# Attention of eight image groups run as one stream of 128 steps

## The chip, the core and the metric

The kernel runs on one core of one Trainium2 chip. The core has five engines that each work through a program of their own, in order: TensorE (PE in the rows, its weight loads PEld), VectorE (DVE), ScalarE (ACT), GpSimd (POOL) and SyncE (SP), which here only issues DMAs. They wait for each other by semaphores alone. TensorE writes to PSUM, eight banks of 128x512 fp32. The metric is the device time of one launch in microseconds (us), the median over runs.

## The reference

```python
proj = einsum('bnf,df->bnd', patchify(x, 16), W) + b          # 32 images, 36 patches of 768 pixels
h = concat([cls, proj], 1) + pos_enc                          # 37 tokens of 256
h = concat([h, txt], 1)                                       # 114 tokens per image
n = layernorm(h)
q, k, v = n @ Wq, n @ Wk, n @ Wv                              # 16 heads of 64
attn = softmax(causal(q k^T / 8)) ; out = attn v
h = h + (n + out @ Wo)
y = moe(layernorm(h))                                         # 8 experts, top 2, capacity 570, gelu MLP of 1024
return h + y
```

All is fp32. Products that need the full accuracy are made in three passes over high and low parts (`halves`: hi*hi, hi*lo, lo*hi); scores, transposes and attn*v are plain fp32.

## The kernel before

The 32 images are taken in 8 groups of 4 (456 tokens). After a prologue (weights split, group 0 embedded and normalised, its V, and its first Q and K) comes the attention phase, and then the eight experts one after the other, which the change does not touch.

**Inside a group.** 16 steps (`PAIRS`), each for two heads and two of the four images: TensorE makes four score matrices (`scores`), VectorE adds the mask and takes the row maximum (L983) and the bias (L987), ScalarE takes the exponential with its row sum (L706), VectorE inverts the sum (L991), GpSimd multiplies `pr` by it (L573), TensorE transposes the four (`transpose_probs`, `pT_bank`), ScalarE copies them to `pT` (L700), TensorE multiplies by V (`weigh_values`, `o_bank`), and ScalarE and VectorE store the high and low parts `oT_hi`, `oT_lo` (L696, L784). The transposes of a step are made two steps later and the products with V three steps later, so that a group has 16 + 3 rounds of the loop: in the first two no transposes, in the last three no scores.

**Other work, put between the steps of a group by fixed numbers.** In the first 13 rounds a chunk of the projections Q or K of this group for a later step (128x456, six matmuls, `project`); `E` (the embedded patches of the next group transposed), `Y` and `L` (the normalised output of the last group transposed, and the router's logits), `X` (tokens of the next group transposed) and V of the next group (8 blocks of six 512-wide matmuls, `project_v`). Behind the last round stand `embed` of the group after the next (32 matmuls into a score bank), `count_places`, the output projection `project_o` of the group (96 matmuls, 256 wide) and then Q0, K0 and Q1 of the next. All these small jobs go round three PSUM banks: `claim` waits until the job three places before was emptied by ScalarE or VectorE.

**The residual** `hx = hraw + xn` of a group is one buffer. GpSimd writes it in two halves (L583), the first only when the output projection of the last group has been taken.

**The pixels.** SyncE waits for both halves of `hx` (they free `hraw`), loads the text of the next group, then the pixels of the group after it (12 DMAs, L398), waits for them and shifts them in SBUF with two more (L406). ScalarE's `pack` (L645) waits for these and reorders the pixels for `embed`. In the kernel before it stands in step 10 of a group.

**Dispatch.** The router's result of a group is computed by VectorE in six parts (`route`), and GpSimd writes its rows to DRAM by 8 indirect DMAs (`dispatch`, L554), all of them between two groups.

Of the kernel before, what the change touches and what calls it, by code (L numbers as in the profile page):

```python
# [17 lines left out]
F32 = mybir.dt.float32  # L18
# [14 lines left out]
D = 256  # L33
# [37 lines left out]
def build(nc, x, txt, tokW, tok_b, cls_token, pos_enc, Wq, Wk, Wv, Wo,  # L71
          router_w, router_b, w1, b1, w2, b2, out, slots):
    ctx = ExitStack()
    with ctx:
# [41 lines left out]
        hx = place("hx", [T, GB, D])  # L116
# [13 lines left out]
        x2T = nc.alloc_sbuf_tensor_at("x2T", [128, KC, GT], F32, offset=x2T_at)  # L130
        rows = [place(f"rows{i}", [T, GB, ROW]) for i in range(2)]
# [66 lines left out]
        def psum(name):  # L198
# [17 lines left out]
        embedded, embT_done, packed = sem("embedded"), sem("embT_done"), sem("packed")  # L216
# [24 lines left out]
        START = ([("W", "d")] * 4 + [("E", "d")] * 2 + [("X", "ad")] * 2  # L241
                 + [("V", "a"), ("V", "d")] * GB + [("Q", "d"), ("K", "a"), ("Q", "d"), ("B", "d")])
# [9 lines left out]
        STATS2, MOMENTS2, NORM2 = {1: (0, 1), 2: (2, 3)}, 3, {5: (0, 1), 6: (2, 3)}  # L252
        STATS1, MOMENTS1, NORM1 = {7: (0, 1), 8: (2, 3)}, 8, {10: (0, 1), 11: (2, 3)}
        AT_RSTD1, AT_RSTD2 = 9, 4
        AT_PACK = 10

        ROUTE_AT = {AT_L + 3: 1, PAIRS: 2, PAIRS + 1: 3, PAIRS + 2: 4}

        LAST_QK = PAIRS - 3

        def next_qk(n):

            return "KQ"[n % 2], n // 2 + 1 + n % 2

        def body_jobs(first, last):
            jobs = []
            for n in range(PAIRS + 3):
                if n < LAST_QK:
                    jobs.append(next_qk(n) + (("a", "d")[n % 2],))
                if not last and n == AT_E:  # L270
                    jobs += [("E", 0, "d"), ("E", 1, "d")]
                if not first and n == AT_Y:
                    jobs += [("Y", 0, "a"), ("Y", 1, "d")]
                if not first and n == AT_L:
                    jobs.append(("L", 0, "d"))
                if not last and n == AT_X:
                    jobs += [("X", 0, "ad"), ("X", 1, "ad")]
                if not last:
                    jobs += [("V", 2 * b, "a") for b in V_FIRST.get(n, ())]
                    jobs += [("V", 2 * b + 1, "d") for b in V_SECOND.get(n, ())]  # L280
            if not first:
                jobs.append(("C", 0, "d"))
            jobs += [("O", 0, "d"), ("O", 1, "d")]
            if not last:
                jobs += [("Q", 0, "d"), ("K", 0, "a"), ("Q", 1, "d")]
            return jobs

        START_JOBS = []
        seen = {}
        for name, by in START:  # L290
            START_JOBS.append((name, seen.get(name, 0), by))
            seen[name] = seen.get(name, 0) + 1
        END_JOBS = [("Y", 0, "a"), ("Y", 1, "d"), ("L", 0, "d"), ("C", 0, "d")]
        FIRST, STEADY, LAST = body_jobs(True, False), body_jobs(False, False), body_jobs(False, True)
# [3 lines left out]

        ALL_JOBS = START_JOBS + FIRST + STEADY * (G - 2) + LAST + END_JOBS

        class Jobs:


            def __init__(self, where):
                self.seq = ALL_JOBS
                if where == "start":
                    self.at = 0
                elif where == "end":
                    self.at = len(ALL_JOBS) - len(END_JOBS)
                else:  # L310
                    self.at = len(START_JOBS) + (len(FIRST) + (where - 1) * len(STEADY) if where else 0)

            def index(self, name, k):
                for i in range(self.at, len(self.seq)):
                    if self.seq[i][:2] == (name, k):
                        return i
                raise KeyError((name, k))

            def bank(self, name, k):
                return bank[self.index(name, k) % len(bank)]  # L320

            def total(self, i, engine=None):
                return count(self.seq[:i + 1], engine)

            def last_before(self, name, k):

                return max(i for i in range(self.at) if self.seq[i][:2] == (name, k))

            def filled(self, name, k):
                return self.total(self.index(name, k))  # L330

            def emptied(self, i):

                sems = {"a": act_drained, "d": dve_drained}
                return [(sems[e], self.total(i, e)) for e in self.seq[i][2]]

            def drained(self, name, k):
                return self.emptied(self.index(name, k))

            def bank_free(self, name, k):  # L340

                i = self.index(name, k) - len(bank)
                return self.emptied(i) if i >= 0 else []


# [25 lines left out]
        def pair(g, n):  # L371
            return g * PAIRS + n
# [18 lines left out]
        def _(sp):  # L391
# [48 lines left out]
            def body(g, first=False, last=False):  # L440
                jobs = Jobs(g)
                if not last:
                    sp.wait_ge(hx_done, 2 * g + 2)
                    load_text(g + 1)
                if g < G - 2:
                    sp.wait_ge(packed, g + 2)
                    load_pixels(g + 2)
                if first:
                    clear_slots()
                if not first:  # L450
                    wait_all(sp, jobs.emptied(jobs.last_before("O", 1)))
                    set_out(g - 1)

            body(0, first=True)
            for g in range(1, G - 2):
                body(g)
            body(G - 2)
            body(G - 1, last=True)
            jobs = Jobs(G - 1)
            wait_all(sp, jobs.drained("O", 1))  # L460
# [15 lines left out]
            jobs = Jobs("end")  # L476
            wait_all(sp, [(filled, jobs.filled("L", 0))])
# [19 lines left out]
        def _(pool):  # L497
# [68 lines left out]
            def body(g, first=False, last=False):  # L566
                for n in range(PAIRS + 1):
                    if n >= 1:

                        m = n - 1  # L570
                        after((recip_done, pair(g, n)))
                        for i in range(4):
                            p = pool.tensor_scalar(pr[:, m % 4, i, :], pr[:, m % 4, i, :], rc[:, m % 4, i:i + 1], 1.0, ALU.mult, ALU.mult)  # L573
                        p.then_inc(normed, 1)
                    if n in (0, 1):

                        if first and n == 0:
                            after((xn_done, GB))
                        elif n == 0:
                            jobs = Jobs(g)  # L580
                            after((xn_done, GB * (g + 1)), *jobs.emptied(jobs.last_before("O", 1)))
                        b = slice(2 * n, 2 * n + 2)
                        pool.tensor_tensor(hx[:, b, :], hraw[:, b, :], xn[:, b, :], ALU.add).then_inc(hx_done, 1)  # L583
                    if n == AT_RSTD2 and not first:
                        rstd(g - 1, vareps2, rstd2_done, ve2, rstd2)
                    if n == AT_RSTD1 and not last:
                        rstd(g + 1, vareps1, rstd1_done, ve1, rstd1)
                if not first:
                    for i in range(TOPK * GB):
                        dispatch(g - 1, i)  # L590

            body(0, first=True)
            for g in range(1, G - 1):
                body(g)
            body(G - 1, last=True)
# [18 lines left out]
        def _(act):  # L614
# [7 lines left out]
            def drain(jobs, name, k, dst, src, **kw):  # L622
                act.wait_ge(filled, jobs.filled(name, k))
                act.activation(dst, src, ACT.Copy, **kw).then_inc(act_drained, 1)  # L624

            def drain_x(jobs, k):
                drain(jobs, "X", k, xT_hi[:, k, :], jobs.bank("X", k)[:, 0:GT])

            def drain_k(jobs, c):
                drain(jobs, "K", c, kT[:, c % 2, :], jobs.bank("K", c)[:, 0:GT])  # L630

            def drain_v(jobs, b):
                drain(jobs, "V", 2 * b, vv[:, b, 0:512], jobs.bank("V", 2 * b)[0:T, :])

            def drain_y(jobs):
                drain(jobs, "Y", 0, x2T[:, 0, :], jobs.bank("Y", 0)[:, 0:GT])
# [20 lines left out]
            for k in range(KC):  # L657
                drain_x(jobs, k)
# [746 lines left out]
```

## Time and profile before

| | us |
|---|---|
| median of 3 runs | 954.19 (951.41 to 954.93) |
| the profiled execution | 953.52 |
| its span | 951.6 |
| first scores of group 0 | 51.82 |
| first scores of groups 1 and 2 | 133.48 and 214.02 |
| first scores of group 7 | 612.25 |
| output projection of group 7 starts | 665.84 |
| TensorE busy | 869.6 (91% of the span) |
| VectorE, ScalarE, GpSimd busy | 556.2, 516.0, 370.5 |

Times in the rows are us from the start of the span. A row of the timeline is a run of equal instructions: its start, how long it lasted, engine, line, operation, tiles and count, and in brackets how long the engine stood idle before it and which instruction ended that. Matmuls overlap: the next one starts before the last has ended, so that the step from start to start is what one costs. The PEclk column is the TensorE clock that was granted, 1.00 for 2.4 GHz and 0.50 for 1.2 GHz.

### The profile page before, as it was taken

The page shows a single profiled execution, that of the slowest core. Times are in us where ns is not written, and L with a number is a line of the kernel's source. Part 1 is how long each engine was busy: PE and PEld are TensorE (multiplying, and loading weights), DVE is VectorE, ACT ScalarE, POOL GpSimd, SP SyncE. Part 2 cuts the span into 40 slices and gives each one's busy share as a digit, 9 for nine tenths or more (in the row PEclk, how much of TensorE's full clock was granted, in tenths as well). Part 3 has the DMA queues.
Part 4 walks back from the last instruction along what each step waited for, and adds up shares of the span by engine and source line. Part 5 has one row for each costly group of instructions (what it writes and reads, how often), then busy time and mean ns, then how long its engine had stood idle before and what let it go on. Part 6 is the DMA issues. An engine that isn't in the chain of part 4 may idle for free.

```text
span 951.6 us, 19817 instructions
## 1 busy us (share of the span) xinstructions
PE 869.6 (91%) x6897; PEld 754.2 (79%) x6897; DVE 556.2 (58%) x2433; ACT 516.0 (54%) x1686; POOL 370.5 (39%) x677
## 2 busy tenths in 40 slices
PE   4898999999999999999999999997708999999996
PEld 4676787797788778779777877875708999999996
DVE  3566347528645753863775485476236767777761
ACT  3368438807824961880684386186016555565551
POOL 2134225345425424543542653554430333322333
PEclk8799899999999999999999999998758999999999
DMA  8224302012002101200200200100135655444322
GB/s 252 50 58 132 98 13 60 2 41 74 1 8 65 43 1 42 71 2 22 68 16 1 59 9 2 38 2 1 24 100 179 158 117 134 102 121 121 83 26 25
DMA packets 61908, 57.64 MB, mean 61 GB/s; under 512 B 26784, under 2 KB 56652, under 8 KB 61697
## 3 DMA queue, kind: packets, MB, share of 16 engines
q1 hardware_dynamic: 41170, 45.15, 15.5%
q0 software_dynamic: 18944, 9.76, 6.5%
q10 hardware_dynamic: 1696, 1.49, 0.6%
q8 instruction: 55, 0.90, 0.4%
q14 instruction: 43, 0.34, 0.1%
HBM read 34.25 MB, written 21.89 MB: 59 GB/s over the span
## 4 chain that ended last, share of the span: by engine, by line
PE 82%; DVE 4%; POOL 4%; issue 4%; ACT 3%; DMA 1%; SPq 1%; POOLq 0%; DVEq 0%; ACTq 0%
PE bank L380 14%; PE bank L382 13%; PE bank L381 13%; PE pT_bank L1241 6%; PE score_bank L1232 6%; PE o_bank L1252 6%; PE score_bank L1130 4%; POOL pr L573 2%; PE o_bank L381 2%; PE o_bank L382 2%; PE o_bank L380 2%; PE score_bank L380 2%; PE score_bank L381 2%; PE score_bank L382 2%; ACT pr L706 2%
## 5 line engine op out<-in xcount | busy, mean ns | idle before, releaser
L573 POOL TENSOR_SCALAR pr<-pr,rc 114x114 f32<-114x114 f32 x512 | 179.7, 371 | 233.7 <-DVE rc L991 233.7
L706 ACT ACTIVATE pr<-sm,nb 114x114 f32<-114x114 f32 x512 | 192.1, 379 | 22.6 <-DVE nb L987 21.2
L983 DVE CUSTOM_DVE_ANT_0 sm<-score_bank,mask 114x114 f32<-114x114 f32 x512 | 110.5, 272 | 55.2 <-PE score_bank L1232 55.2
L604 POOL DMA_INDIRECT out_dram<-yout,dest x40 | 74.0, 1849 | 163.0 <-ACT yout L758 161.5
L554 POOL DMA_INDIRECT slots_dram<-rows,slot x64 | 72.8, 1137 | 128.2 <-DVE slot L950 93.3
L624 ACT ACTIVATE kT<-bank 128x456 f32<-128x456 f32 x64 | 34.1, 532 | 146.8 <-PE bank L382 146.8
L380 PE MATMUL bank<-xT_hi,wqkv_hi 128*128 128x456 f32 x256 | 103.5, 404 | 0.0
L1232 PEld LDWEIGHTS score_bank<-kT,qT 64*114 64x114 f32 x1024 | 62.1, 177 | 45.5 <-issue 35.3
L706 ACT ACTIVATION_READ_ACCUMULATOR pr<-sm,nb 114x1 f32 x512 | 97.0, 189 | 0.0
L381 PE MATMUL bank<-xT_lo,wqkv_hi 128*128 128x456 f32 x256 | 94.3, 368 | 0.0
L382 PE MATMUL bank<-xT_hi,wqkv_lo 128*128 128x456 f32 x256 | 94.3, 368 | 0.0
L1232 PE MATMUL score_bank<-kT,qT 64*114 64x114 f32 x1024 | 84.8, 284 | 9.1 <-DVE mx L983 6.0
L1241 PE MATMUL pT_bank<-ident,pr 114*114 114x114 f32 x512 | 78.1, 276 | 10.2 <-POOL pr L573 10.2
L700 ACT ACTIVATE pT<-pT_bank 114x456 f32<-114x456 f32 x128 | 70.5, 551 | 23.4 <-PE pT_bank L1241 23.2
L1252 PE MATMUL o_bank<-pT,vv 114*64 114x114 f32 x1024 | 79.2, 276 | 2.3 <-ACT pT L700 2.1
L1241 PEld LDWEIGHTS pT_bank<-ident,pr 114*114 114x114 f32 x512 | 49.6, 136 | 30.4 <-POOL pr L573 14.0
L380 PE MATMUL bank<-wo_hi,oT_hi 128*114 128x256 f32 x256 | 73.4, 287 | 0.0
L382 PE MATMUL bank<-wo_hi,oT_lo 128*114 128x256 f32 x256 | 72.8, 284 | 0.0
L381 PE MATMUL bank<-wo_lo,oT_hi 128*114 128x256 f32 x256 | 72.7, 284 | 0.0
L696 ACT ACTIVATE oT_hi<-o_bank 128x228 fp32r<-128x228 f32 x128 | 45.7, 357 | 47.3 <-PE o_bank L1252 47.3
L1252 PEld LDWEIGHTS o_bank<-pT,vv 114*64 114x64 f32 x1024 | 50.9, 137 | 22.9 <-issue 8.1
L784 DVE TENSOR_TENSOR oT_lo<-o_bank,oT_hi 128x228 fp32r<-128x228 f32 x128 | 47.9, 374 | 34.0 <-ACT oT_hi L696 33.5
(198 smaller groups left out, 2228.1 us busy)
## 6 DMA issues: line engine op xcount, KB each, us to landing
stage_a<-in_L_ffn_w_dram SPq DMA_DIRECT2D x8, 1024.0 KB, 5.0
stage_b<-in_L_ffn_w_dram SPq DMA_DIRECT2D x8, 1024.0 KB, 7.1
slots_dram<-fill SPq DMA_DIRECT2D x8, 605.6 KB
xs<-slots_dram SPq DMA_DIRECT2D x8, 605.6 KB
pix<-in_x_dram SPq DMA_DIRECT2D x96, 36.0 KB, 2.3
hraw<-in_txt_dram SPq DMA_DIRECT2D x8, 308.0 KB
out_dram<-h SPq DMA_DIRECT2D x8, 308.0 KB
pix<-pix SPq DMA_DIRECT2D x7, 216.0 KB, 2.6
```

What stands on the lines that cost most here:

```text
L380: pe.matmul(out_ap, a[0], b[0], start=start, stop=False)
L381: pe.matmul(out_ap, a[0], b[1], start=False, stop=False)
L382: return pe.matmul(out_ap, a[1], b[0], start=False, stop=stop)
L554: pool.indirect_dma_start(slots, bass.IndirectOffsetOnAxis(ap=slot[:, j, b:b + 1], axis=0), rows[k % 2][:, b, :], None, bounds_check=E * C ...
L573: p = pool.tensor_scalar(pr[:, m % 4, i, :], pr[:, m % 4, i, :], rc[:, m % 4, i:i + 1], 1.0, ALU.mult, ALU.mult)
L604: pool.indirect_dma_start(out, bass.IndirectOffsetOnAxis(ap=dest[e % 2][:, t:t + 1], axis=0), yout[:, t, :], None, compute_op=ALU.add).the ...
L700: act.activation(pT[:, m % 2, :, :], pT_bank[0:T, 0:4 * T].rearrange("p (i q) -> p i q", i=4), ACT.Copy).then_inc(pT_copied, 1)
L706: a = act.activation(pr[:, n % 4, i, :], sm[:, n % 2, i, :], ACT.Exp, bias=nb[:, n % 2, i:i + 1], scale=SCALE, accum_out=rs[:, n % 4, i:i ...
L983: m = dve.tensor_tensor_reduce(sm[:, n % 2, i, :], score_bank[i % 2][0:T, i // 2 * T:(i // 2 + 1) * T], mask[:, :], 1.0, NEG, ALU.add, ALU ...
L1232: m = pe.matmul(score_bank[h][0:T, b * T:(b + 1) * T], qT[head, c % 2, tokens], kT[head, c % 2, tokens], start=True, stop=True)
L1241: m = pe.transpose(pT_bank[0:T, i * T:(i + 1) * T], pr[:, n % 4, i, :], ident[0:T, 0:T])
L1252: m = pe.matmul(o_bank[n % 2][h * DK:(h + 1) * DK, b * T:(b + 1) * T], vv[:, b0 + b, v0:v0 + DK], pT[:, n % 2, 2 * b + h, :], start=True, ...
```

## The change

The loops over groups and over the steps in one are replaced by one loop over 128 steps N (group g, step n), plus four rounds to drain it. There are no rounds without scores between two groups, and the transposes of a step are now made three steps later (`LAG_T`), the products with V four (`LAG_O`).

- A chunk of Q or K stands in every one of the 16 steps; those of steps 13, 14 and 15 are of the next group.
- The second halves of V (`V2` below, 4 blocks) of a group are made in its own steps 5 to 8; of the first halves three stand in steps 14 and 15 of the group before and one in step 0. In the prologue only the first halves of group 0 are left.
- The output projection of the last group stands in steps 4 and 5, half each. Its input `oT` is still one buffer, so that in these two steps ScalarE's and VectorE's high and low parts (`late`) wait for it and stand at the end of the step.
- `embed` is in step 9, in one of the three banks. `E` is in step 6, `Y` in 10, `L` in 11, `X` in 13.
- `pack` is moved from step 10 to step 4, behind the late part. Both halves of `hx` are now written in steps 1 and 2, into two buffers in turn.
- The dispatches of a group stand in steps 4 to 11 of the group after the next, one in each.

TensorE makes the same matmuls as before, and no engine has other instructions than before.

```diff
-        AT_E, AT_Y, AT_L, AT_X = 3, 8, 12, 13
-        V_FIRST = {AT_X + 1: (0,), AT_X + 2: (1, 2), AT_X + 3: (3,)}
-        V_SECOND = {PAIRS + 1: (0, 1), PAIRS + 2: (2, 3)}
-        AT_PACK = 10
+        LAG_T, LAG_O = 3, 4
+        AT_O, AT_V2, AT_E, AT_M, AT_Y, AT_L, AT_X = 4, 5, 6, 9, 10, 11, 13
+        AT_PACK, AT_RSTD1, AT_RSTD2 = 4, 10, 8
+        NORM1 = {11: (0, 1), 12: (2, 3)}
...
-                    if n in (0, 1):
-                        if first and n == 0:
-                            after((xn_done, GB))
-                        elif n == 0:
-                            after((xn_done, GB * (g + 1)), *jobs.emptied(jobs.last_before("O", 1)))
+                if g < G and n in (1, 2):
+                    if n == 1:
+                        pool.wait_ge(xn_done, GB * (g + 1))
+                        if g > 1:
+                            wait_all(pool, drained("O", 2 * g - 3))
...
+                late = n in (LAG_O, LAG_O + 1)
+                if N >= LAG_O and not late:
+                    take_outputs(N - LAG_O)
+                if LAG_T <= N < STEPS + LAG_T:
+                    m = N - LAG_T
+                    act.wait_ge(pT_done, m + 1)
+                    act.activation(pT[:, m % 2, :, :], ...).then_inc(pT_copied, 1)
...
+                if N >= LAG_O and late:
+                    take_outputs(N - LAG_O)
+                if g + 2 < G and n == AT_PACK:
+                    pack(g + 2)
...
+            for N, g, n in steps():
+                if n == AT_X and g + 1 < G:
+                    transpose_tokens("X", g + 1, xn, xn_done)
+                if N < STEPS:
+                    scores(N)
+                if N >= LAG_O:
+                    weigh_values(N - LAG_O)
+                if LAG_T <= N < STEPS + LAG_T:
+                    transpose_probs(N - LAG_T)
+                if g < G:
+                    if chunk_at(g, n):
+                        project(*chunk_at(g, n))
+                    for f, b in value_jobs(g, n):
+                        project_v(f, b, 0)
+                    if n - AT_V2 in range(GB):
+                        project_v(g, n - AT_V2, 1)
+                    if n == AT_E and g + 1 < G:
+                        transpose_patches(g + 1)
+                    if n == AT_M and g + 2 < G:
+                        embed(g + 2)
+                    if g > 0:
...
+                        if n - AT_O in range(2):
+                            project_o(g - 1, n - AT_O)
```

TensorE at the start of a group, before: the last matmul of the output projection of group 0, then the last matmul of Q0, K0, Q1, and the first three steps of group 1 (L1232 scores, L1241 transposes, the rest a chunk of Q or K).

```order
L382 MATMUL bank<-wo_hi,oT_lo 114x256
...
L382 MATMUL bank<-xT_hi,wqkv_lo 128x456
L1232 MATMUL score_bank<-kT,qT 114x114 x4
L380 MATMUL bank<-xT_hi,wqkv_hi 128x456
...
L1232 MATMUL score_bank<-kT,qT 114x114 x4
L380 MATMUL bank<-xT_hi,wqkv_hi 128x456
...
L1232 MATMUL score_bank<-kT,qT 114x114 x4
L1241 MATMUL pT_bank<-ident,pr 114x114 x4
```

After: TensorE in step 5 of group 1, with the end of the output projection's first half before it, a chunk of K, one V2 block and the second half, and then the start of step 6.

```order
L361 MATMUL bank<-wo_hi,oT_lo 114x256
L1166 MATMUL score_bank<-kT,qT 114x114 x4
L1187 MATMUL o_bank<-pT,vv 64x114 x4
L1175 MATMUL pT_bank<-ident,pr 114x114 x4
L359 MATMUL bank<-xT_hi,wqkv_hi 128x456
...
L359 MATMUL bank<-wqkv_hi,xT_hi 114x512
...
L359 MATMUL bank<-wo_hi,oT_hi 114x256
...
L1166 MATMUL score_bank<-kT,qT 114x114 x4
```

The output projection has gone from between two groups, where nothing of attention stood beside it, into two steps with scores, products and transposes.

ScalarE in group 0, before: from the exponentials of step 9 past `pack` of group 2 (L645) into step 11.

```order
L700 ACTIVATE pT<-pT_bank 114x456
L706 ACTIVATE pr,rs<-sm,nb 114x114 x4
L696 ACTIVATE oT_hi<-o_bank 128x228
L700 ACTIVATE pT<-pT_bank 114x456
L706 ACTIVATE pr,rs<-sm,nb 114x114 x4
L645 ACTIVATE tok<-pix 96x1152
L624 ACTIVATE kT<-bank 128x456
```

After: from the exponentials of step 3 past the same `pack` (now L610) into step 5.

```order
L673 ACTIVATE pr,rs<-sm,nb 114x114 x4
L588 ACTIVATE kT<-bank 128x456
L667 ACTIVATE pT<-pT_bank 114x456
L673 ACTIVATE pr,rs<-sm,nb 114x114 x4
L648 ACTIVATE oT_hi<-o_bank 128x228
L610 ACTIVATE tok<-pix 96x1152
L667 ACTIVATE pT<-pT_bank 114x456
L673 ACTIVATE pr,rs<-sm,nb 114x114 x4
```

`pack` is six steps earlier in the group, and the copy of the transposed probabilities of step 2 now stands right behind it.

## Rows read from the trace of the kernel before

**Rows 1.** Busy time by engine over the stream of group 0 and of group 1
```profile
core 0: us, PE busy (x) PEld busy (x) DVE busy (x) ACT busy (x) POOL busy (x), PEclk, DMA share, GB/s
51.82:133.48 81.66, 78.27 (x610) 63.69 (x610) 39.01 (x209) 46.55 (x175) 25.91 (x67) 0.96 0.28 84
133.48:214.02 80.54, 78.14 (x635) 64.26 (x635) 47.33 (x252) 47.35 (x177) 36.22 (x76) 1.00 0.13 34
```

**Rows 2.** Timeline of TensorE in group 1: two of its idle times
```profile
169.14 0.66 PE L1232 MATMUL score_bank<-kT,qT 64*114 64x114 f32 x8 [0.51 <-ACT kT L624]
...
176.97 0.66 PE L1232 MATMUL score_bank<-kT,qT 64*114 64x114 f32 x8 [0.64 <-DVE mx L983]
```

**Rows 3.** Timeline of TensorE in group 1: one plain step, to the next scores
```profile
153.23 0.66 PE L1232 MATMUL score_bank<-kT,qT 64*114 64x114 f32 x8
153.81 0.61 PE L1252 MATMUL o_bank<-pT,vv 114*64 114x114 f32 x8
154.36 0.60 PE L1241 MATMUL pT_bank<-ident,pr 114*114 114x114 f32 x4
154.73 0.45 PE L380 MATMUL bank<-xT_hi,wqkv_hi 128*128 128x456 f32 x1
...
156.13 0.56 PE L1232 MATMUL score_bank<-kT,qT 64*114 64x114 f32 x6
```

**Rows 4.** Timeline of TensorE: starts of V blocks, L, X, embed and the output projection
```profile
41.96 0.39 PE L380 MATMUL bank<-wqkv_hi,xT_hi 128*114 128x512 f32 x1
...
43.35 0.40 PE L380 MATMUL bank<-wqkv_hi,xT_hi 128*114 128x512 f32 x1
...
172.06 1.67 PE L1265 MATMUL bank<-router_sb,x2T 128*114 128x8 f32 x16
173.59 1.08 PE L1150 MATMUL bank<-ident,xn 114*128 114x114 f32 x8
174.60 0.66 PE L1232 MATMUL score_bank<-kT,qT 64*114 64x114 f32 x8
...
194.76 4.08 PE L1130 MATMUL score_bank<-tok,embW 96*128 96x144 f32 x32
...
198.76 0.35 PE L380 MATMUL bank<-wo_hi,oT_hi 128*114 128x256 f32 x1
...
210.19 0.38 PE L380 MATMUL bank<-xT_hi,wqkv_hi 128*128 128x456 f32 x1
```

**Rows 5.** Timeline of all engines in group 0: residual, pixel DMAs and pack
```profile
55.90 1.40 POOL L573 TENSOR_SCALAR pr<-pr,rc 114x114 f32<-114x114 f32 x4 [20.59 <-DVE rc L991]
...
57.27 1.27 POOL L583 TENSOR_TENSOR hx<-hraw,xn 114x512 f32<-114x512 f32 x1
...
57.58 0.99 DVE L987 TENSOR_SCALAR nb<-mx 114x4 f32<-114x4 f32 x1
...
66.67 2.09 SPq L406 DMA_DIRECT2D pix<-pix  x2
...
84.07 2.19 ACT L645 ACTIVATE tok<-pix 96x1152 f32<-96x1152 f32 x1
```

**Rows 6.** DMA issues of the page: KB each, median us to landing
```profile
pix<-pix SPq DMA_DIRECT2D x7, 216.0 KB, 2.6
```

**Rows 7.** Timeline of TensorE in group 0: its longest idle time
```profile
94.38 1.12 PE L1232 MATMUL score_bank<-kT,qT 64*114 64x114 f32 x8 [2.11 <-DVE mx L983]
```

**Rows 8.** Busy time by engine in the stretches behind that idle time
```profile
94.30:98.00 3.70, 3.62 (x22) 2.99 (x23) 2.01 (x14) 2.53 (x11) 2.61 (x8) 0.50 0.42 130
98.00:102.00 4.00, 4.00 (x27) 2.75 (x25) 1.03 (x10) 2.46 (x11) 0.18 (x1) 0.68 0.42 131
```

**Rows 9.** Timeline of TensorE: scores of step 13 of group 7, last product, output projection
```profile
650.90 0.66 PE L1232 MATMUL score_bank<-kT,qT 64*114 64x114 f32 x8
...
662.76 1.03 PE L1252 MATMUL o_bank<-pT,vv 114*64 114x114 f32 x8 [0.64 <-ACT pT L700]
...
665.84 0.54 PE L380 MATMUL bank<-wo_hi,oT_hi 128*114 128x256 f32 x1
```

More of the change, by code:

```diff
@@ L296, in count @@
+        JOB_AT = {job[:2]: i for i, job in enumerate(JOBS)}
         def count(jobs, engine=None):
             return sum(1 for j in jobs if engine is None or engine in j[2])
[L299 to L343, printed above, removed]
@@ L369, in ebank_free, with steps @@
             return [{"H": (gelu_done, NF * f + n + 1), "S": (xs_done, NX * f + n + 1), "Y": (y_done, CT * f + n + 1)}[was]]
-        def pair(g, n):
-            return g * PAIRS + n
+        STEPS = PAIRS * G
+        def steps():
+            for N in range(STEPS + LAG_O):
+                yield (N,) + divmod(N, PAIRS)
         def wait_all(eng, waits):
@@ L596, in _ @@
+            for i in range(TOPK * GB):
+                dispatch(G - 2, i)
             rstd(G - 1, vareps2, rstd2_done, ve2, rstd2)
@@ L722, in _ @@
+            drain_y(G - 1)
             router_exp(G - 1)
@@ L1045, in _ @@
+                if N >= LAG_O and late:
+                    give_low_outputs(N - LAG_O)
+            for i in range(2):
+                drain_o(G - 1, i)
+                dve.wait_ge(dve_drained, drained_by("O", 2 * (G - 1) + i, "d"))
+                for b in (2 * i, 2 * i + 1):
+                    statistics(b, h2, st2, stats2)
             moments(G - 1, st2, mv2, stats2, moments2)
@@ new lines, in count_places, with scores @@
+            def count_places(k):
+                pe.wait_ge(routed, ROUTE_STEPS * k + sum(ROUTE_PARTS[:5]))
+                dst = claim("C", k)[0:T, 0:GB * E]
+                pe.matmul(dst, upto[:, :], chosen[:, :, :], start=True, stop=False)
+                pe.matmul(dst, ones[:, :], before[:, 0:GB, :], start=False, stop=True).then_inc(filled, 1)
+            def scores(N):
+                n = N % PAIRS
+                c, b0 = N // 2, 2 * (n % 2)
+                if b0 == 0:
+                    wait_all(pe, drained("K", c))
+                    wait_all(pe, drained("Q", c))
+                if N > 0:
+                    pe.wait_ge(max_done, N)
@@ new lines, in _ @@
+            wait_all(pe, drained("W", 3))
+            embed(0)
+            transpose_patches(0)
+            transpose_tokens("X", 0, xn, xn_done)
+            tokens_split(0)
+            pe.wait_ge(wv_lo, 1)
+            for b in range(GB):
+                project_v(0, b, 0)
+            pe.wait_ge(wk_lo, 1)
+            project("K", 0)
+            pe.wait_ge(wq_lo, 1)
+            project("Q", 0)
+            project("K", 1)
+            embed(1)
+            pe.wait_ge(b1_in, 16)
+            dst = claim("B", 0)
@@ L1297, in body @@
                         if n == AT_Y:
[L1298 to L1300 removed]
+                            transpose_tokens("Y", g - 1, rows[(g - 1) % 2], xn2_done)
                         if n == AT_L:
[L1302 to L1307 removed]
@@ L1308, in body @@
-                if not last and not (isinstance(g, int) and g == G - 2):
-                    embed(g + 2)
-                if not first:
-                    count_places(jobs, g - 1)
-                if first:
-                    pe.wait_ge(wo_lo_done, 1)
-                pe.wait_ge(o_lo, pair(g, PAIRS))
-                for k in range(2):
-                    project_o(jobs, k)
-                if not last:
-                    project(jobs, "Q", 0)
-                    project(jobs, "K", 0)
-                    project(jobs, "Q", 1)
@@ L1335, in e_claim @@
+                if n == AT_C and g > 1:
+                    count_places(g - 2)
+            for i in range(2):
+                project_o(G - 1, i)
+            transpose_tokens("Y", G - 1, rows[(G - 1) % 2], xn2_done)
+            logits(G - 1)
+            count_places(G - 1)
             def e_claim(name, e, k):
```

697 lines of the change are left out of this document (301 added, 396 removed).

## The prediction

> **What bounds the kernel now.** I read the page first: TensorE is busy for 91% of the span and no other engine for more than 58%. Then the windows by stage. From the first scores of group 1 to those of group 2 TensorE is busy for 78.14 us of 80.54 at the full clock, beside 47.3 us of VectorE and of ScalarE and 36.2 us of GpSimd [rows 1]. So in the attention phase only TensorE counts. An idle 2.4 us is the first thing that a better order can give back in a group. The timeline shows what ends it: in two of its four pieces, 0.51 us until ScalarE has stored K and 0.64 us until VectorE has taken the row maxima [rows 2]. The other two wait for GpSimd's `pr`. Group 0 is worse: 3.4 us idle and a mean clock of 0.96 [rows 1].
>
> **What a group costs when nothing waits.** Start to start, a plain step is 156.13 - 153.23 = 2.90 us: scores 0.58, products with V 0.55, transposes 0.37, a chunk 1.40 [rows 3]. A V block is 43.35 - 41.96 = 1.39, `embed` and the two small matmuls behind it 198.76 - 194.76 = 4.00, the output projection 210.19 - 198.76 = 11.43, L 1.53, X 1.01 [rows 4]. Y and E have X's shape or nearly, and I take 0.85 for each; behind a chunk L, X, E or Y saves a change back of some 0.08. The new group holds 16 plain steps 46.4, 8 V blocks 11.1, `embed` and C 4.0, output projection 11.4, and L, X, Y, E 4.1 together: 77.0 us. That is 3.5 below 80.54: 2.4 is the idle time, 1.1 the changes of operand and of tile in the three rounds without scores and in the first two steps, which are gone.
>
> **What the new order puts in its place.** I followed each queue through the steps with the durations above.
> - Step 6: the second E job needs the bank that Q of the same step filled, and VectorE stores that only in step 7. It begins step 6 late, since the low part of step 5's output waits for the second half of the output projection; then come a V2 block, an output half, the maxima, a low part and two statistics, together about 5.1 us behind the start of step 6, where TensorE asks at 4.6: 0.5 us.
> - Steps 12 to 14: VectorE normalises the last two images in step 12 behind the router's first part, about 0.5 us too late for X in step 13, and K of step 13 waits some 0.3 us for the low part of X. The maxima of step 13 are late as well, but a chunk now stands ahead of the next scores, so the 0.64 us [rows 2] are covered.
> - Steps 4 and 5: `oT` is single, so its writers wait for TensorE. Nothing on TensorE needs them before step 6, and each half projection is 5.7 us long.
>
> That makes 1.3 us a group. It is bounded by 0 (all covered) and by 3.5 (each of these queues is late by about as much as in the old order, and the gain is eaten). I take 1.3, since each part comes from a row-by-row count and VectorE has 30 us to spare in a group.
>
> The dispatches now run beside VectorE. While GpSimd added `hx` from 57.27 to 58.54, VectorE's `nb`, 4 elements wide, took 0.99 us and ended with it [rows 5]: the two block one another. At most that adds 1 us to a step's VectorE work in 8 steps of 16; in steps 4 to 11 TensorE mostly needs 3.6 us or more, and the transposes have a whole step more of slack, so I put it at 0 with the bound above. By the Trainium skill ("SBUF — State Buffer", section Who interferes with whom) the shared port pair is an exclusive lock, and a DMA from GpSimd's queue can wait for VectorE to get its descriptors written; by that rule the dispatch could be late as well as `nb`, each time by one VectorE instruction. The sum by the row has `nb` alone late; by the rule the dispatches are too, and both leave it at 940.8, since GpSimd has 40 us spare in a group and nobody in the phase waits for a dispatch; only the bound of 3.5 us a group would be reached more easily.
>
> **The early pack in group 0.** This is the large term against the change. The pixels for group 2 are asked for when both halves of `hx` are written. Before, the second half ended at 57.27 + 1.27 = 58.54, 6.7 us after the first scores at 51.82. Now it stands behind `pr` of step 1 as well as the first half: 1.40 + 1.27 more, and ends 9.4 to 9.5 us after them. From there the load and the shift were issued by 66.67 + 2.09 = 68.76 [rows 5]; landing takes 2.6 from an issue [rows 6], the last of which began at about 68.2, so the pixels are there 12.2 us after the residual: 21.7 us after the first scores. `pack` then takes 2.19 [rows 5], and the copy of step 2's transposes behind it 0.55: 24.4 us. TensorE wants that copy in step 6. It gets there after three steps of 2.04 (scores and a chunk, with the changes between them), one of 2.36 with transposes, one of 2.90, one of 4.29 with V2, and the scores of step 6: 16.3 us. It stands for 8.1 us. `pack` was in step 10 before, at 84.07, 13 us after its pixels were in.
>
> After 2.11 us of idle time [rows 7] the granted clock was 0.50 for 3.7 us and 0.68 for the next 4.0 [rows 8], which is 3.7 x 0.50 + 4.0 x 0.32 = 3.1 us of work; part of the slow stretch is also ScalarE catching up, so I take 2.5. Together 10.6 us, bounds 0 (the pixels come sooner) and 14.
>
> In groups 1 to 5 the same chain ends about 24 us after the first scores, but there `pack` stands beside the output projection: step 6 starts 31.7 us after them (4.3 + 3 x 2.9 + 8.6 + 10.0). After 2.7 us for `pack` and copy some 5 us are left. I cost it at nothing; if that cover goes, the price is what comes above 5 us, per group.
>
> **The sum.** The prologue has four V blocks less: 4 x 1.39 = 5.6, first scores at 51.82 - 5.56 = 46.3. VectorE's weight splits still lie beside the rest. Group 0: 46.4, less 3 x 0.37 and 4 x 0.55 for the empty pipeline, plus 7 V blocks 9.7, E 0.9, `embed` 3.9, X 0.8: 58.5. Then groups 1 to 5 at 77.0, group 6 without `embed` 73.1, and group 7 to its step 13: 13 x 2.9 + 5 x 1.39 + 11.4 + Y, L, C 2.3 = 58.4. So these scores start at 46.3 + 58.5 + 385.0 + 73.1 + 58.4 = 621.3, plus 10.6 for the early pack, plus 6 x 1.3 + 0.5 for the waits: 640.2, against 650.90 [rows 9]: 10.7 earlier.
>
> The tail: the last three steps are bound by the chain through ScalarE and GpSimd as before. The output projection started at 665.84, 3.1 us behind the last products at 662.76 [rows 9], since it waited for the router's count and for the last low part. Now the count is a step earlier and the first half asks only for the last step but one: it starts when the products are done, about 2 us sooner. All behind it follows. The dispatches of group 6 still stand ahead there, but start sooner as well.
>
> In all 10.7 + 2.0 = 12.7 us less. The profiled execution took 953.52 (span 951.6 and 1.9 around it), 0.7 below the median 954.19. So its like would take 940.8, the median 941.5, and I say 941.5.
>
> **Rivals.**
> - *No stall in group 0.* The pixels come before TensorE needs the copy, or something I don't see hides it. For it: the DMA engines are lightly loaded. Against: it is SyncE's issue of 14 DMAs that takes the 10 us, not the bytes. 941.5 - 10.6 = 931. Chance 0.12.
> - *The waits move instead of going.* VectorE and ScalarE, in order, pass the late parts on, and dispatches block VectorE, so that a group loses the whole 3.5 us: 6 x 2.2 = 13 us back. 954.5, no change. For it: the three banks are tight in steps 5 to 7 and VectorE's queue there is full. Against: 30 us of slack a group. Chance 0.10; half of it on the way there (about 948) 0.08.
> - *Slower: the pack isn't covered in groups 1 to 5 either.* Place: step 6 of each, TensorE waiting for the copy behind `pack`. It decides once the pixels land over 5 us later than I reckon; each further us costs 5, and any gap of 2 us or more brings the clock's 3 us with it. At 8 us late: 5 x (3 + 2.5) = 28, 969. For it: group 0 does just this. Against: the load of each group is the same 14 DMAs, and the cover is made of the two halves of the output projection, whose length a row gives [rows 4]. Chance 0.06.
> - My forecast, 937 to 946 by itself: 0.64.
>
> The range that leaves out 2 in 10: 931 to 949. A measurement of this kernel tells 0.5%, 4.8 us, from no change. Faster than 949.4: 0.64 + 0.12 + 0.06 of the halfway case = 0.82; same (to 959) 0.12; slower 0.06.
>
> **What would show it.** First scores of group 0 at 46.3. An idle time of TensorE of 8 us ahead of the products of step 6 in group 0, released by ScalarE's copy with `pack` ahead of it, and the clock at 0.50 behind it. First scores of group to group 78.3 us apart, idle some 1.3, ended by VectorE in steps 6 and 13. In groups 1 to 5 `pack` ends before step 6. Output projection of group 7 right behind the last products. I am wrong if the groups are 80 us apart, if the large idle time returns in every group, or if group 0 has none.

## The result, and the profile after

| | before | after |
|---|---|---|
| median, runs on one chip | 954.02 (951.38 to 954.93), 7 runs | 947.86 (945.23 to 948.27), 7 runs |
| ratio | | 0.9939 [0.9923, 0.9955] |
| the profiled execution, its span | 953.52, 951.6 | 947.86, 945.7 |
| first scores of groups 0, 1, 2 | 51.82, 133.48, 214.02 | 46.76, 117.73, 195.83 |
| periods of groups 2 to 5, group 6 | 80.57, 75.96 | 78.92 to 78.99, 75.02 |
| scores of step 13 of group 7 | 650.90 | 645.93 |
| last product, output projection | 662.76, 665.84 | 660.16, 661.11 |

The change makes the kernel 6.2 us faster. The forecast of 941.5 is 12.5 below the same median, so the time lies inside the range but the gain is a little less than half of what was said.

The page of the kernel after; TensorE is busy for nearly as long as before (866.3 us against 869.6), in a span 5.9 us shorter:

```profile
span 945.7 us, 19862 instructions
...
PE 866.3 (92%) x6897; PEld 759.8 (80%) x6897; DVE 562.7 (60%) x2433; ACT 519.1 (55%) x1686; POOL 373.2 (39%) x677
```

The windows of groups 0, 1 and 2, from first scores to first scores, the view of [rows 1]:

```profile
46.76:117.73 70.97, 61.76 (x464) 48.94 (x463) 36.03 (x203) 42.54 (x166) 24.38 (x63) 0.93 0.32 97
117.73:195.83 78.10, 77.26 (x634) 64.64 (x633) 43.39 (x235) 47.80 (x177) 26.90 (x68) 1.00 0.09 23
195.83:274.75 78.92, 77.38 (x635) 64.91 (x634) 48.76 (x252) 47.84 (x177) 36.84 (x76) 1.00 0.13 35
```

TensorE's idle time fell from 2.4 us in a group of 80.5 to 0.8 in group 1 and 1.5 in group 2. Group 0 is 71 us long, but 9.2 of them are idle and its mean clock is 0.93. The waits view says what all of it was. These are all waits of TensorE from 46 to 646 us (engine, tile and line, who released it, us in total, times, longest):

```profile
PE o_bank L1187 <- ACT pT L667: 8.5, 1, 8.5
PE bank L359 <- issue: 5.8, 7, 0.8
PE score_bank L1166 <- DVE mx L951: 4.2, 6, 0.7
```

Three waits, 18.5 us, each always in the same place. The document goes through them one after the other.

**The single wait of 8.5 us** is in group 0, step 6. TensorE's timeline, then ScalarE's, then the windows behind the wait:

```profile
62.48 0.66 PE L1166 MATMUL score_bank<-kT,qT 64*114 64x114 f32 x8
71.61 1.03 PE L1187 MATMUL o_bank<-pT,vv 114*64 114x114 f32 x8 [8.48 <-ACT pT L667]
```

```profile
68.98 2.14 ACT L610 ACTIVATE tok<-pix 96x1152 f32<-96x1152 f32 x1 [9.32 <-DMA pix<-pix]
71.03 0.53 ACT L667 ACTIVATE pT<-pT_bank 114x456 f32<-114x456 f32 x1
```

```profile
71.61:74.50 2.89, 2.89 (x15) 2.50 (x16) 1.18 (x5) 2.79 (x12) 0.00 (x0) 0.50 0.41 133
74.50:78.00 3.50, 3.50 (x11) 2.60 (x10) 1.76 (x12) 1.60 (x8) 1.39 (x4) 0.58 0.42 132
78.00:82.00 4.00, 4.00 (x37) 3.29 (x35) 3.19 (x14) 1.73 (x7) 0.87 (x3) 1.00 0.42 131
```

The releaser named is the copy, but read one row up: what it copies was there before 62.48, and it stood behind `pack`, which waited 9.32 us for the pixels. The copy started 24.3 us behind the first scores and ended 24.8 us behind them. Afterwards TensorE ran at 1.2 GHz (0.50) and was back at 2.4 by 78.0: 2.9 x 0.50 + 3.5 x 0.42 = 2.9 us of work.

**The six waits of 0.70 us**, one in each of groups 2 to 7: TensorE, VectorE and GpSimd at the end of step 3 of group 2.

```profile
209.69 0.66 PE L1166 MATMUL score_bank<-kT,qT 64*114 64x114 f32 x8 [0.70 <-DVE mx L951]
```

```profile
207.19 0.17 DVE L904 SCALAR_TENSOR_TENSOR sl<-pick,ps__114 114x8 f32<-114x8 f32 x1
207.28 1.29 DVE L906 TENSOR_SCALAR over<-ps__114 114x8 f32<-114x8 f32 x1
208.60 0.17 DVE L908 SCALAR_TENSOR_TENSOR slot<-sl,over 114x8 int32<-114x8 f32 x1
208.68 0.27 DVE L951 CUSTOM_DVE_ANT_0 sm<-score_bank,mask 114x114 f32<-114x114 f32 x1
```

```profile
207.25 1.28 POOL L551 TENSOR_TENSOR hx<-hraw,xn 114x512 f32<-114x512 f32 x1
```

The router's fifth part stands ahead of the maxima in VectorE's step 3. Its `over`, 8 elements wide like its neighbours of 0.17, lasts 1.29 and ends when GpSimd's second half of `hx` does (208.57 and 208.53).

**The seven waits of 0.84 us** (0.73 in group 0) stand ahead of K of step 13 in groups 0 to 6. TensorE and VectorE in group 1:

```profile
184.45 0.45 PE L359 MATMUL bank<-xT_hi,wqkv_hi 128*128 128x456 f32 x1 [0.84 <-issue]
```

```profile
182.64 1.17 DVE L745 TENSOR_TENSOR xT_lo<-bank,xT_hi 128x456 fp32r<-128x456 f32 x2 [1.59 <-ACT xT_hi L588]
183.73 0.62 DVE L749 COPY qT<-bank 128x456 f32<-128x456 f32 x1
```

"Issue" says only that the profile names no releaser; the queues show it. K of step 13 takes the bank that Q of step 12 filled; VectorE was idle for 1.59 us, nearly all of it with that Q ready, since the low parts of X, which wait for ScalarE, stand ahead of it. K starts 0.10 us after the store of Q ends (183.73 + 0.62 = 184.35).

**The end of the stream.** TensorE from the scores of step 13 of group 7 on:

```profile
645.93 0.66 PE L1166 MATMUL score_bank<-kT,qT 64*114 64x114 f32 x8
...
649.38 0.66 PE L1166 MATMUL score_bank<-kT,qT 64*114 64x114 f32 x8
650.47 0.61 PE L1187 MATMUL o_bank<-pT,vv 114*64 114x114 f32 x8 [0.43 <-ACT pT L667]
...
652.64 0.61 PE L1187 MATMUL o_bank<-pT,vv 114*64 114x114 f32 x8 [1.03 <-ACT pT L667]
...
654.94 1.03 PE L1187 MATMUL o_bank<-pT,vv 114*64 114x114 f32 x8 [1.16 <-ACT pT L667]
...
657.55 1.03 PE L1187 MATMUL o_bank<-pT,vv 114*64 114x114 f32 x8 [0.64 <-ACT pT L667]
...
660.16 1.03 PE L1187 MATMUL o_bank<-pT,vv 114*64 114x114 f32 x8 [0.52 <-ACT pT L667]
...
661.11 0.56 PE L359 MATMUL bank<-wo_hi,oT_hi 128*114 128x256 f32 x1
```

From the start of the last scores to that of the last products it is 10.78 us, where the kernel before took 662.76 - 654.86 = 7.90: the stream now has four rounds to drain, not three, and in each the products wait for ScalarE's copy. The output projection then starts 0.95 us after the last products start, not 3.1 [rows 9].

### The profile page after: what moved, and what is told of

Same layout as the page of the kernel before. It is cut to its first block, busy times and chain, and to the rows that moved or that the text cites. A ratio compares the mean times of both kernels' runs of the same rounds, so it can differ in the third digit from the quotient of the medians.

```text
span 945.7 us, 19862 instructions
## 1 busy us (share of the span) xinstructions
PE 866.3 (92%) x6897; PEld 759.8 (80%) x6897; DVE 562.7 (60%) x2433; ACT 519.1 (55%) x1686; POOL 373.2 (39%) x677
## 3 DMA queue, kind: packets, MB, share of 16 engines
q1 hardware_dynamic: 41170, 45.15, 15.7%
## 4 chain that ended last, share of the span: by engine, by line
PE 83%; DVE 7%; issue 4%; DMA 2%; POOL 2%; ACT 1%; SPq 1%; POOLq 0%; DVEq 0%
PE bank L359 14%; PE bank L360 13%; PE bank L361 13%; PE score_bank L1166 7%; PE o_bank L1187 6%; PE pT_bank L1175 6%; PE bank L1081 4%; PE o_bank L360 2%; PE o_bank L361 2%; PE o_bank L359 2%; PE score_bank L359 2%; PE score_bank L360 2%; PE score_bank L361 2%; PE bank L1101 2%; DVE sm L951 2%
## 5 line engine op out<-in xcount | busy, mean ns | idle before, releaser
L359 PE MATMUL bank<-xT_hi,wqkv_hi 128*128 128x456 f32 x256 | 105.2, 411 | 5.8 <-issue 5.8
L524 POOL DMA_INDIRECT slots_dram<-rows,slot x64 | 75.6, 1181 | 36.1 <-DVE slot L908 19.8
L1175 PE MATMUL pT_bank<-ident,pr 114*114 114x114 f32 x512 | 78.5, 277 | 0.0
L1187 PEld LDWEIGHTS o_bank<-pT,vv 114*64 114x64 f32 x1024 | 51.4, 138 | 26.8 <-ACT pT L667 13.5
L359 PE MATMUL bank<-wo_hi,oT_hi 128*114 128x256 f32 x256 | 72.6, 284 | 0.0
L745 DVE TENSOR_TENSOR hid_lo<-gl,hid_hi 128x282 fp32r<-128x282 f32 (+1 forms) x128 | 58.4, 456 | 4.4
```

Source lines behind the costliest of these rows:

```text
L359: pe.matmul(out_ap, a[0], b[0], start=start, stop=False)
L524: pool.indirect_dma_start(slots, bass.IndirectOffsetOnAxis(ap=slot[:, j, b:b + 1], axis=0), rows[k % 2][:, b, :], None, bounds_check=E * C ...
L745: dve.tensor_tensor(lo, whole, hi.bitcast(F32), ALU.subtract).then_inc(done, 1)
L1175: p = pe.transpose(pT_bank[0:T, i * T:(i + 1) * T], pr[:, m % 4, i, :], ident[0:T, 0:T])
L1187: p = pe.matmul(o_bank[m % 2][h * DK:(h + 1) * DK, b * T:(b + 1) * T], vv[:, b0 + b, v0:v0 + DK], pT[:, m % 2, 2 * b + h, :], start=True, ...
```

## The experiments

All edit the kernel after. They ran on two chips, on which the kernel before took 954.02 us (experiments 1 to 4) and 952.34 us (5 to 8), so each is given by its ratio to the kernel before on the same chip; 0.0010 is 0.95 us, and the kernel after stands at 0.9939. Beside it stands what the trace of one execution gives from the first scores of group 0 to the end of the span, which leaves the prologue out: its length ran from 45.15 to 47.36 us over the nine traces of this order, with the same instructions in it but for experiment 5. The kernel after has 945.7 - 46.76 = 898.9 there.

**1. Pack of group 2 later, in group 0 alone.**

```diff
-                if g + 2 < G and n == AT_PACK:
+                if g + 2 < G and n == (8 if g == 0 else AT_PACK):
                     pack(g + 2)
```

> The changed kernel with one pack moved: that of group 2, which stands in group 0, from step 4 to step 8; the others stay in step 4. Theory (the copy behind the early pack holds TensorE, and the clock falls with it): the idle time of 8.5 us in step 6 of group 0 and the slow matmuls behind it go, 11 us in all, so 936.9 against 947.9; first scores of groups 0 and 1 about 60 us apart instead of 71. Rival (TensorE would have stood there anyway, for the load of the pixels or for ScalarE's backlog): the idle time only moves to step 9 or 10 and the time changes by less than 3 us.

Measured: 935.98 (935.39 to 937.38), ratio 0.9815 [0.98, 0.9831]: 11.9 us faster than the kernel after; by the trace 888.2, 10.7 less. The window of group 0, then TensorE's waits from 45 to 640 us:

```profile
47.17:106.86 59.69, 58.96 (x465) 46.89 (x464) 36.07 (x203) 42.62 (x166) 24.47 (x63) 1.00 0.35 105
```

```profile
PE bank L359 <- issue: 5.8, 7, 0.8
PE score_bank L1166 <- DVE mx L951: 4.3, 6, 0.7
PE o_bank L1187 <- ACT pT L667: 0.4, 1, 0.4
```

The large wait and the slow clock are gone, group 0 is 70.97 - 59.69 = 11.3 us shorter, and the two small waits are untouched (the last row is the first wait of the drain). So the wait did not move to a later step. Of the 11.3 the trace as a whole keeps 10.7: groups 1 to 6 together are 0.2 longer and the stretch behind the scores of step 13 of group 7 is 0.4 longer, which is no more than two executions may differ by.

**2. The store of Q ahead of the low parts of X on VectorE.**

```diff
-                    if n == AT_X and g + 1 < G:
-                        drain_x(g + 1)
                     if n % 2 == 1 and chunk_at(g, n - 1):
                         drain_q(chunk_at(g, n - 1)[1])
+                    if n == AT_X and g + 1 < G:
+                        drain_x(g + 1)
```

> The changed kernel with VectorE's queue of step 13 in another order: the chunk of Q made in step 12 is stored before the low parts of X and not behind them. Theory (TensorE's wait of 0.84 us ahead of K of step 13 is for this store): the wait falls to about 0.3 us in each of 7 groups, 3.8 us less, 944.1. Rival (it waits for the low part of X alone, which ScalarE's exponentials make late): 947.9, nothing changes.

Measured: 943.66 (941.92 to 945.35), ratio 0.9894 [0.9877, 0.991], 4.2 us faster than the kernel after; by the trace 895.2, 3.7 less. The waits are now `PE bank L359 <- issue: 2.0, 7, 0.3`, and the periods of groups 2 to 5 78.4 to 78.5. So it was the store of Q; the 0.3 left is K waiting for the low parts of X themselves (in group 2 they end at 262.21 and K starts at 262.31), the amount that the prediction had named.

**3. The router's fifth part behind the maxima.**

```diff
-                if n == AT_C + 1 and g > 1:
-                    route(g - 2, 5)
...
-                if g > 1 and n in ROUTE_NEXT and n != AT_C + 1:
+                if g > 1 and n in ROUTE_NEXT:
                     route(g - 2, ROUTE_NEXT[n])
```

> The changed kernel with the router's last part moved on VectorE from ahead of the maxima of step 3 to the end of step 3. Theory (this part, 1.0 us by itself and 2.1 with GpSimd's block, is what makes the scores of step 4 wait 0.70 us): the wait goes in groups 2 to 7, 6 x 0.7 = 4.2 us less, 943.7. Rival (VectorE's queue is late as a whole there, and the wait turns up in the next step or at the bank of the output projection): less than 1 us.

Measured: 942.99 (941.91 to 943.43), ratio 0.989 [0.9872, 0.9908], 4.9 us faster than the kernel after; by the trace 894.7, 4.3 less. The six waits are gone, the periods 78.2. In this kernel `over` has a mean of 0.16 us, and in its place `nb` of step 3 lasts 0.94 at 205.72, beside the same half of `hx`: the stretched instruction stays, on another victim that TensorE does not wait for.

**4. The drain with transposes ahead of products.** ScalarE's copy stands ahead of its high part there in the same way.

```diff
-                if N >= LAG_O:
+                if LAG_O <= N < STEPS:
                     weigh_values(N - LAG_O)
                 if LAG_T <= N < STEPS + LAG_T:
                     transpose_probs(N - LAG_T)
+                if N >= STEPS:
+                    weigh_values(N - LAG_O)
```

> The changed kernel with the four rounds behind the last scores in another order: transposes before products on TensorE, and the copy of the transposes before the output's high part on ScalarE. Theory (the one step more of lag made the drain a chain of four times product, transpose, copy, 2.2 to 2.6 us each, 10.8 us from the last scores to the last product against 7.9 before): the last product comes 7.9 to 8.5 us after the last scores, 2.5 us less, 945.4. Rival (the chain through exponentials and GpSimd sets the end of the drain): nothing changes, 947.9.

Measured: 946.05 (944.9 to 947.36), ratio 0.9921 [0.9906, 0.9937], 1.8 us faster than the kernel after, within the uncertainty of the two; by the trace 897.9, 1.1 less. From the last scores to the last product it takes 656.74 - 647.23 = 9.51 us, 1.27 less. The drain is still 1.6 longer than before, and 7.9 to 8.5 was expected: the transposes now wait for ScalarE's copy in their turn (1.11 and 0.95 us), and from 652.65 on a set of them takes 0.98 instead of 0.60, so the slow clock is still there.

**5. The halves of the residual a step earlier.** Experiment 3 doesn't tell the length of part five from GpSimd's hold on VectorE. This one leaves VectorE's order alone.

```diff
-                if g < G and n in (1, 2):
+                if g < G and n in (0, 1):
...
-                    b = slice(2 * n - 2, 2 * n)
+                    b = slice(2 * n, 2 * n + 2)
                     pool.tensor_tensor(hx[g % 2][:, b, :], hraw[:, b, :], xn[:, b, :], ALU.add).then_inc(hx_done, 1)
```

> The two halves of the residual hx are added by GpSimd in steps 0 and 1 of a group instead of 1 and 2; nothing else moves. It tests two things. First, group 0: the pixels for group 2 are asked for when the second half is written, so that the idle time of TensorE ahead of the products of step 6 should shrink from 8.48 us by what the residual comes earlier, one step of about 2.8 us, to about 5.7; the slow clock behind it stays. If the stall were set by the length of the transfer or by pack itself, it would stay at 8.5. Second, groups 2 to 7: the wait of 0.70 us of the scores of step 4 for the row maxima. My theory is that the last GpSimd half (207.25, 1.28 us) stretches VectorE's 8-wide over from 0.17 to 1.29 us; then over takes about 0.17 again, and the wait is gone (6 x 0.7 = 4.2 us). The rival is that the router's fifth part, standing ahead of the maxima, is late by its own length: then the wait stays at 0.7. Theory: 947.9 - 2.8 - 4.2 = 941. Rival: 945. If neither moves: 948.

Measured: 940.1 (939.29 to 941.65) against 952.34, ratio 0.9871 [0.9853, 0.9889], 6.5 us faster than the kernel after; by the trace 891.5, 7.5 less. TensorE's waits from 45 to 640 us, and `over` of group 2:

```profile
PE o_bank L1187 <- ACT pT L667: 6.2, 1, 6.2
PE bank L359 <- issue: 5.8, 7, 0.8
```

```profile
203.44 0.17 DVE L906 TENSOR_SCALAR over<-ps__114 114x8 f32<-114x8 f32 x1
```

Both parts of the theory hold. Part five still stands ahead of the maxima, and the 0.70 us are gone with GpSimd's addition. The addition now meets another instruction of VectorE, which TensorE doesn't wait for:

```profile
195.46 1.28 POOL L551 TENSOR_TENSOR hx<-hraw,xn 114x512 f32<-114x512 f32 x1
195.48 1.31 DVE L885 TENSOR_TENSOR oh<-io,pick 114x32 f32<-114x32 f32 x1
```

And the stall of group 0 shrank by 2.3 us (5.7 was expected, 6.19 measured) as the residual came earlier: its second half ends 52.67 - 45.95 = 6.7 us behind the first scores instead of 56.29 - 46.76 = 9.5. So the stall is dated by the residual, not by the length of the transfer alone. The 2.8 did not come back whole, since SyncE's twelve loads of pixels took 8.52 us instead of 8.04.

**6. The four edits of 1 to 4 together.**

> Four edits together: pack of group 2 in step 8 of group 0, VectorE's store of Q ahead of the low parts of X in step 13, the router's fifth part at the end of VectorE's step 3, and the drain with transposes ahead of products. Alone they gave 11.9, 4.2, 4.9 and 1.8 us against the kernel after the change (947.86). If they act in different places and nothing else comes to bind, they add: 947.9 - 22.8 = 925.1, ratio to the kernel before 0.970. The rival is that they share part of their gain (a wait that one removes was given back at the next by the other): then 929 to 932. Periods of the groups from 2 on about 77.7 us.

Measured: 927.85 (927.32 to 929.21) against 952.34, ratio 0.9741 [0.9726, 0.9756]. That is 18.9 us below the kernel after, and 2.6% faster than before. By the medians (0.9741 x 954.02 = 929.3) that is the rival's figure, 3.9 short of the 22.8. The trace says otherwise: 925.3 - 45.57 = 879.7, 19.2 less, where the four alone gave 10.7 + 3.7 + 4.3 + 1.1 = 19.8. By the traces they add within 0.6 us, and the sum of four differences of medians was too large. The periods of groups 2 to 5 are 77.6 to 77.7, as expected. The window of group 2:

```profile
182.41:260.11 77.70, 77.40 (x635) 64.89 (x635) 48.72 (x252) 48.04 (x177) 36.94 (x76) 1.00 0.13 36
```

An idle 0.30 us is left in a group, the K of step 13.

**7. All dispatches of a group in step 5.**

```diff
-                if 1 < g < G and n - AT_DISPATCH in range(TOPK * GB):
-                    dispatch(g - 2, n - AT_DISPATCH)
+                if 1 < g < G and n == AT_DISPATCH + 1:
+                    for i in range(TOPK * GB):
+                        dispatch(g - 2, i)
```

> The eight indirect DMAs of a group's dispatch all stand in step 5 on GpSimd instead of one in each of steps 4 to 11. Each occupies GpSimd for 1.2 to 1.4 us in the trace of the kernel after the change. The prediction put the dispatches at no cost. If that is right, this kernel takes the same time, 947.9, within 1.5 us: the burst of about 10 us lies beside the two halves of the output projection, and the pr of step 4 comes some 3 us late where the transposes are three steps away. The rival is that each dispatch beside the steps holds VectorE up for about a microsecond and so delays maxima in steps 6 to 11 of five or six groups: then taking seven of the eight away from these steps gives back 3 to 10 us (938 to 945).

Measured: 946.79 (946.02 to 948.69) against 952.34, ratio 0.9939 [0.9925, 0.9954], the same as the kernel after; by the trace 898.6, 0.3 less. Its three waits of TensorE are those of the kernel after (8.2, 5.8 and 4.2 us). Spread over eight steps or all in one, the dispatches cost the same.

**8. Pack in step 8 of every group** (`AT_PACK = 8`).

> Pack stands in step 8 in every group instead of step 4, not in group 0 alone. The prediction put pack at no cost in groups 1 to 5, with 5 us of cover by the output projection. If so, this is as fast as the kernel with pack moved in group 0 alone: 935.98, within 1 us, and each group's period is the same. If pack and the copy behind it did cost something in groups 1 to 5 (a share of the 0.65 us a group that the forecast missed), it is up to 5 x 0.6 = 3 us faster, about 933. If step 8 is worse for them, because there pack has only the V2 block and embed beside it (cover of 4.3 us or less against 2.7 for pack and copy), it is slower by 1 to 5 us, 937 to 941.

Measured: 936.62 (935.64 to 937.3) against 952.34, ratio 0.9832 [0.9818, 0.9846], by the trace 888.0 against 888.2 of experiment 1. The intervals of the two ratios overlap, and the traces agree: the same. In the kernel after, the `pack` that stands in group 2 (that of group 4) ends before it can hurt:

```profile
222.61 2.23 ACT L610 ACTIVATE tok<-pix 96x1152 f32<-96x1152 f32 x1 [3.81 <-DMA pix<-pix]
224.73 0.54 ACT L667 ACTIVATE pT<-pT_bank 114x456 f32<-114x456 f32 x1
```

The copy is done at 225.27, and TensorE asks for it at 228.85, behind the scores of step 6. The cover is 3.6 us, and 3.6 to 4.5 in groups 1 to 5, where the prediction reckoned 5. That figure was not a sound one: its chain of 24 us had `pack` and the copy in it, and 2.7 for them were taken off once more. Without this slip 31.7 - 24.4 = 7.3 were left. The true cover is smaller because the chain runs later there: in group 2 the second half of the residual ends 12.7 us behind the first scores, not 9.5, and `pack` starts 26.8 us behind them, not 22.2.

## Why the prediction was half right

**Held, with its size.** The first scores came at 46.76 (forecast 46.3; the prologue by itself varies by 2.2 us, so a hit this close is partly luck). The early pack stopped TensorE for 8.48 us (forecast 8.1), in step 6, group 0 alone, released by the copy behind `pack`; with the clock it cost 11.3 by experiment 1 (forecast 10.6). Groups 1 to 5 covered `pack`, as experiment 8 shows, by less than was reckoned. No wait of TensorE came from the dispatches, and moving seven of the eight changed nothing (experiment 7). The output projection of group 7 follows the last products directly.

**Failed: "That makes 1.3 us a group".** The sum of the prediction for groups 2 to 5 is 77.0 + 1.3 = 78.3; they took 78.95. Two terms make up that 0.65 in each of these groups: the waits gave 0.24 of it and the work itself 0.4.
- The waits were 1.54, not 1.3, and in other places. The wait of the second E job in step 6 (0.5) and that of X in step 13 (0.5) did not come; K of step 13 waited 0.84, not 0.3, because the low parts of X delay the store of Q, which was left out; and the 0.70 of step 4 was not seen at all. It follows from two things that were both in the prediction: that GpSimd's addition of `hx` holds a small VectorE instruction up [rows 5], and that `hx` now stands in steps 1 and 2. The prediction asked this of the dispatches only. The halves start behind `pr`, a step late, and so the second lies beside the router's fifth part in step 3. Group 1 has no router work there and no such wait, and took 78.10.
- What a group costs when nothing waits is 77.40 (experiment 6, idle time taken off), not 77.0. Set step by step beside the prediction's pieces, the trace shows it in two places. `E` takes 219.36 - 218.28 = 1.08 there, where 0.85 less 0.08 was put down without a row. And step 13 takes 250.09 - 246.63 = 3.46 with an idle 0.30, so 3.16 for work instead of 2.90: a wait costs more than its idle time, since the transposes ahead of it take their full 0.60 us, where the next matmul otherwise starts after 0.37.

**Failed: the tail, 2.0 us.** It said that the last steps are bound by the chain "as before", and that only the start of the output projection changes. That start did come 3.1 - 0.95 = 2.1 sooner. But the products now lag by one round more, and the drain is 2.88 us longer. From the scores of step 13 to the output projection it is 15.18, against 14.94 before. 1.7 came back between the start of the projection and the normalised output's transposes (16.95 against 18.68). By the two traces 0.6 of it is TensorE's own time (busy for 13.10 us against 13.70, at a mean clock of 0.90 against 0.87) and 1.1 a shorter wait for VectorE's normalised rows (3.85 against 4.98); no run tests why.

**Counted up.** Ahead of the scores of step 13 of group 7 the forecast was 5.7 us short (645.93 against 640.2): 0.5 in the prologue, 1.9 in group 0 (70.97 against 58.5 + 10.6), 2.6 in groups 2 to 5, about 0.6 in group 6 and 0.4 in group 7, less 0.2 in group 1. Of the 1.9, 0.73 is the wait for K of step 13, 0.7 the stall and the clock, and the remaining 0.4 lies in the 58.5 for the work itself, as in the later groups. Behind those scores it was 1.1 short: the tail gave 0.9 (300.7 against 299.8 to the end), not 2.0. Together 6.8; the execution's 947.86 is 7.1 above 940.8, the other 0.3 being what lies around the span (2.2, not 1.9).

Of the rivals, "the waits move instead of going" is the one that the result resembles, and its halfway figure (948) is the measured one, by luck. Its reason did not hold. The waits left in a group did not come from a general crowding of VectorE and ScalarE but from two pieces of VectorE's queue in a wrong place, and moving them gave back one wait wholly and 0.54 of the other's 0.84. And of the 6.8 us that the forecast was short, most are not waits of the groups at all: work sized too small, the longer drain, the prologue and the clock.

## What to carry to other kernels

When a schedule is rolled over a border, check its first turn apart: there the producers (here pixels behind a residual) are still dated by the prologue, while every later group has covered them, and one in-order instruction behind such a wait stops the whole engine. When a row shows that one engine's instruction blocks another's, ask it of every instruction that moves, not only of the one the change is about. And count what one more step of lag costs where the stream ends, since there nothing covers it.

## What the hardware showed

An addition of 114x512 on GpSimd holds up some small VectorE instructions until it has ended: `over` 0.17 to 1.29, `nb` 0.17 to 0.94 (experiment 3), `oh` to 1.31 (experiment 5). Others beside it kept their length: `sm` 0.27 and the store `qT` 0.63. Moving VectorE's instruction and moving the addition both only changed the victim; each time the new one was one that TensorE doesn't wait for. The other way round it was seen once: in the prologue of experiment 5 the addition lasted 2.98 us instead of 1.28, beside VectorE's `wo_lo` of 2.29 that had started first. The Trainium skill ("SBUF — State Buffer", section Who interferes with whom) calls the shared port pair an exclusive lock held for the whole instruction, and the ends of `over` and of the addition, 208.57 and 208.53, agree. Its other half, that a dispatch from GpSimd could be held up in turn, cost nothing here: experiment 7 moved seven of eight and the time stayed.

An 8.48 us wait of TensorE cost another 2.8 by the slow clock behind it (11.3 in all). The drain's waits are shorter, but from 654.94 to 660.16 TensorE ran at 0.50 as well:

```profile
654.94:660.16 5.22, 4.06 (x27) 3.02 (x27) 3.04 (x16) 1.83 (x4) 1.04 (x4) 0.50 0.00 0
```

No single idle time in or just ahead of it is over 1.16 us, and a set of eight products takes 1.03 instead of 0.61. The two rounds at 0.50 took 2.61 each, the two before them 2.17 and 2.30. The kernel before had ended its drain in this state too: its last products took 1.03 [rows 9].
